# Attention stage: a reciprocal of 16 sums with a broadcast copy, and projections laid one to a slot

## The reference

```python
q = (x @ Wq + bq) ...; k = (x @ Wk + bk) ...; v = (x @ Wv + bv) ...
scores = einsum('bhqd,bhkd->bhqk', q / sqrt(32), k) + attention_bias
scores = where(src_mask, -inf, scores)
probs = softmax(scores, axis=-1)
ctx = einsum('bhqk,bhkd->bhqd', probs, v)
x = x + (ctx @ Wo + bo)
```

## Time and profile before

| | |
|---|---|
| time, median of 3 runs | 2644.94 us (2638.65 to 2649.93) |
| time of the profiled execution | 2651.21 us |
| span of the profiled execution | 2649.4 us |
| attention, first scores of the loop to the last transposes | 895.38 to about 1874.66 us |
| one middle batch (batch 1) | 1012.24 to 1135.09, 122.85 us |
| PE busy over the span | 92% |

### The profile page before, as it was taken

The page is one execution under the profiler, slowest core; times in us unless marked ns, Lnnn a source line. Parts: engine busy times, 40 slices in busy tenths (PEclk is TensorE's granted clock), DMA queues, the critical chain, the costliest instruction groups (busy, mean ns, idle before and its releaser), DMA issues. The chain is left out here.

```text
span 2649.4 us, 44273 instructions
## 1 busy us (share of the span) xinstructions
PE 2447.0 (92%) x16100; PEld 1920.0 (72%) x16100; DVE 1404.1 (53%) x2668; ACT 993.1 (37%) x1977; POOL 979.5 (37%) x806
## 2 busy tenths in 40 slices
PE   5999999999995789898989999998489999999999
PEld 4687787787783567676766667676378888888887
DVE  5354454454454677777677777777453333333322
ACT  4232231232230566666566656566231212111211
POOL 0031332332240565656565657666020122012200
PEclk9999999999997899999999999999789999999999
DMA  5201110110111555454555555545331001100100
GB/s 161 72 33 40 40 38 33 40 53 18 40 40 55 195 158 174 153 179 153 165 166 181 152 164 168 161 144 165 92 111 48 32 16 47 47 23 25 47 32 16
DMA packets 133361, 243.69 MB, mean 92 GB/s; under 512 B 13212, under 2 KB 17452, under 8 KB 133184
## 3 DMA queue, kind: packets, MB, share of 16 engines
q1 hardware_dynamic: 133184, 241.39, 28.4%
HBM read 216.17 MB, written 25.20 MB: 91 GB/s over the span
## 5 line engine op out<-in xcount | busy, mean ns | idle before, releaser
L951 POOL TENSOR_TENSOR at_bias<-at_bias,at_mask 128x512 f32<-128x512 f32 x512 | 587.3, 1173 | 381.0 <-DMA at_bias<-in_fside_Bx16xSxS 343.3
L648 DVE CAST L_hh<-L_hid 128x512 fp32r<-128x512 f32 x256 | 122.5, 478 | 797.9 <-PE L_acc L746 758.4
L487 ACT ACTIVATE L_hid<-L_turn,L_b1c 128x512 f32<-128x512 f32 x256 | 176.5, 690 | 983.9 <-PE L_turn L285 978.8
L283 PE MATMUL L_turn<-L_xth,L_w1h 128*128 128x512 f32 x1024 | 406.7, 397 | 7.7 <-ACT L_hid L487 5.4
L744 PE MATMUL L_acc<-L_w2h,L_hh 128*128 128x512 f32 x1024 | 403.1, 394 | 8.6 <-DVE L_hl L650 8.6
L284 PE MATMUL L_turn<-L_xth,L_w1l 128*128 128x512 f32 x1024 | 400.7, 391 | 0.0
L285 PE MATMUL L_turn<-L_xtl,L_w1h 128*128 128x512 f32 x1024 | 400.2, 391 | 0.0
L746 PE MATMUL L_acc<-L_w2l,L_hh 128*128 128x512 f32 x1024 | 400.1, 391 | 0.0
L745 PE MATMUL L_acc<-L_w2h,L_hl 128*128 128x512 f32 x1024 | 400.0, 391 | 0.0
L982 ACT ACTIVATE at_bias<-at_bias,at_neg_top 128x512 f32<-128x512 f32 x512 | 363.5, 714 | 44.3 <-DVE at_neg_top L1100 44.1
L1100 DVE CUSTOM_DVE_ANT_0 at_bias<-at_score,at_bias 128x512 f32<-128x512 f32 x512 | 333.0, 684 | 55.9 <-issue 29.8
(11 more groups left out here) (201 smaller groups left out, 3116.0 us busy)
## 6 DMA issues: line engine op xcount, KB each, us to landing
at_bias<-in_fside_Bx16xSxS SPq DMA_DIRECT2D x256, 512.0 KB, 3.7
L_xin<-in_x SPq DMA_DIRECT2D x8, 1024.0 KB, 5.4
L_xres<-in_x SPq DMA_DIRECT2D x8, 1024.0 KB, 5.4
at_xin<-x_scratch SPq DMA_DIRECT2D x8, 1024.0 KB, 6.5
at_xres<-x_scratch SPq DMA_DIRECT2D x8, 1024.0 KB, 6.9
L_xin<-x_scratch SPq DMA_DIRECT2D x8, 1024.0 KB, 5.5
L_xres<-x_scratch SPq DMA_DIRECT2D x8, 1024.0 KB, 5.5
x_scratch<-L_xres SPq DMA_DIRECT2D x7, 1024.0 KB, 4.3
```

The costliest lines, as they stand in the source:

```text
L283: nc_mm = pe.matmul(out, ah, bh, start=i == 0, stop=False)
L487: nc.scalar.activation(hid[m % 2][:, :], turn[m % 2][:, :], func, bias=b1c[:, m:m + 1]).then_inc(h_act, 1)
L951: nc.gpsimd.tensor_tensor(tile, tile, mask[:, m % TT, :], ALU.add).then_inc(masked, 1)
```

## The change

1. `inverse` becomes two instructions: a reciprocal of 128 x 16 sums into a new tile inv, and, after a wait of DVE on its own semaphore, a copy that repeats each of the 16 values 32 times into the 128 x 512 tile. PE's `over` waits on the copy (spread_set).
2. The tables: OUTS puts one output in slot 1, one in slot 2 and two in slot 3. The keys of head tile 1 move from slot 0 to slot 15 of the batch before (KEYS 15: (5, 0), for batch 0 ahead of the loop), its queries from slot 1 to slot 0. VALUES begin in slot 9, which had none, and leave slot 15.
3. TURNS goes. The four k slices of the next x are turned at the end of slot 7 (slice 0, turn[1]), behind unit 1 of slot 8 (slice 1, into gen) and at the end of slot 8 (slices 2 and 3, turn[0] and turn[1]); ACT's and DVE's `turn_hi` and `turn_lo` take their places in slots 8 and 9. Slot 9, which turned slices 2 and 3, now multiplies.

```diff
-    KEYS = {0: (1, 0), 1: (1, 1), 4: (2, 0), 5: (2, 1), 6: (3, 0), 7: (3, 1), 10: (4, 0), 11: (4, 1)}
-    OUTS = {2: (0, 1), 3: (2, 3)}
-    TURNS = {8: (0, 1), 9: (2, 3)}
-    VALUES = {12: 0, 13: 1, 14: 2, 15: 3}
+    KEYS = {0: (1, 1), 4: (2, 0), 5: (2, 1), 6: (3, 0), 7: (3, 1), 10: (4, 0), 11: (4, 1), 15: (5, 0)}
+    OUTS = {1: (0,), 2: (1,), 3: (2, 3)}
+    VALUES = {9: 0, 12: 1, 13: 2, 14: 3}
...
-                of = sums[:, phase * PHASE:(phase + 1) * PHASE].unsqueeze(2).to_broadcast([P, PHASE, HD])
-                nc.vector.reciprocal(spread, of).then_inc(inv_set, 1)
+                nc.vector.reciprocal(inv[:, :], sums[:, phase * PHASE:(phase + 1) * PHASE]).then_inc(inv_set, 1)
+                dve.wait_ge(inv_set, b * PHASES + phase + 1)
+                nc.vector.tensor_copy(spread, inv[:, :].unsqueeze(2).to_broadcast([P, PHASE, HD])).then_inc(spread_set, 1)
...
             def over(b, phase):
-                pe.wait_ge(inv_set, b * PHASES + phase + 1)
+                pe.wait_ge(spread_set, b * PHASES + phase + 1)
...
+                elif m == 8 and j == 1 and not last:
+                    pe.wait_ge(nat_lo, nat_count(b, 3, 1))
+                    turn_x(b + 1, 1, gen)
...
             scores(0, 0, True)
+            pe.wait_ge(v_out, TT - 1)
+            project(0, 1, 0, ALL, gen)
...
-                    if m in TURNS and not last:
-                        pe.wait_ge(pt_even, b * (UNITS // 2) + 2 * m + 2)
-                        pe.wait_ge(pt_odd, b * (UNITS // 2) + 2 * m + 2)
-                        for k in TURNS[m]:
-                            turn_x(b + 1, k)
                     if m % TT == TT - 1:
                         over(b, m // TT)
+                    if m == 7 and not last:
+                        pe.wait_ge(pt_odd, b * (UNITS // 2) + 2 * m + 2)
+                        turn_x(b + 1, 0, turn[1])
+                    if m == 8 and not last:
+                        pe.wait_ge(pt_even, b * (UNITS // 2) + 2 * m + 2)
+                        turn_x(b + 1, 2, turn[0])
+                        pe.wait_ge(pt_odd, b * (UNITS // 2) + 2 * m + 2)
+                        turn_x(b + 1, 3, turn[1])
```

More of the change, by code:

```diff
@@ L1005, in _ @@
             for k in range(KT):
-                turn_hi(0, k)
+                turn_hi(0, k, turn[k % 2])
             split_weights(1)
@@ L1025, in body @@
                     before = m - 1
+                    if m == 8 and not last:
+                        turn_hi(b + 1, 0, turn[1])
+                    if m == 9 and not last:
+                        turn_hi(b + 1, 2, turn[0])
+                        turn_hi(b + 1, 3, turn[1])
                     if before in KEYS:
@@ L1030, in body @@
                         elif not last:
[L1031 to L1034, removed]
+                            nat_hi_of(b + 1, tile - KT, query, gen)
+                    if m == 0:
+                        nat_hi_of(b, 1, 0, gen)
                     if before in VALUES and not last:
                         values(b + 1, 1 - odd, VALUES[before], gen)
-                    if m == 0 and not first:
-                        values(b, odd, TT - 1, gen)
                     after = following(b, m, last)
@@ L1042, in body @@
                         exp(*after, 0)
+                    if m == 8 and not last:
+                        turn_hi(b + 1, 1, gen)
+                    if after:
                         exp(*after, 1)
@@ L1144, in body @@
                     before = m - 1
+                    if m == 8 and not last:
+                        turn_lo(b + 1, 0, turn[1])
+                    if m == 9 and not last:
+                        turn_lo(b + 1, 2, turn[0])
                     if before in KEYS:
@@ L1149, in body @@
                         elif not last:
-                            nat_lo_of(b + 1, 0, query, gen)
+                            nat_lo_of(b + 1, tile - KT, query, gen)
+                    if m == 0:
+                        nat_lo_of(b, 1, 0, gen)
                     if before in OUTS and not first:
-                        output(b - 1, OUTS[before][1], gen)
-                    if before in TURNS and not last:
-                        turn_lo(b + 1, TURNS[before][0])
+                        output(b - 1, OUTS[before][-1], gen)
                     if after:
                         scores(*after, 0)
-                    if before in TURNS and not last:
-                        turn_lo(b + 1, TURNS[before][1])
+                    if m == 9 and not last:
+                        turn_lo(b + 1, 3, turn[1])
                     if after:
@@ L1169, in body @@
                         scores(*after, 2)
-                    if m in OUTS and not first:
+                    if m == 8 and not last:
+                        turn_lo(b + 1, 1, gen)
+                    if m in OUTS and len(OUTS[m]) == 2 and not first:
                         output(b - 1, OUTS[m][0], gen)
@@ L1314, in beside @@
                         gen_free(b, m, first)
-                    if j < 2:
+                    if len(OUTS[m]) == 1:
+                        output(b - 1, OUTS[m][0], some, gen)
+                    elif j < 2:
                         output(b - 1, OUTS[m][0], range(6 * j, 6 * j + 6), gen)
```

52 lines of the change are left out of this document (27 added, 25 removed).

## The result

| | |
|---|---|
| changed kernel, median of 5 | 2576.23 us (2573.42 to 2580.99) |
| kernel before, median of 5 in all | 2645.56 us (2638.65 to 2649.93) |
| ratio | 0.974, 95% interval 0.9721 to 0.9759 |
| profiled execution: time, span | 2573.42 us, 2571.6 us |
| attention, first scores of the loop to the last outputs' first matmul | 895.70 to 1796.51 us |

The change is 2.6% faster. The windows divide the gain: batch 0 takes 105.28 instead of 116.86 (11.6 less), batches 1 to 6 take 692.2 (1000.98 to 1693.20) instead of 744.3 (52.1 less), and batch 7 up to its outputs about 103.3 instead of 118.1 (14.8 less). They add up to 78.5; the other stages are as they were.

A forecast was written before the change was run, and what follows sets the result against it. PE was taken as the bound, with its idle and slow time to win. Gains of 59 + 12 + 10 = 81, less 12 for the clock, gave 69 us: 2582 profiled, 2576 on the median's scale, range 2555 to 2605.

The forecast's parts named there:

- the sum of 69: Whole run: 59 from six middle batches, 12 first batch, 10 last, less 12 for the clock, in us.
- Slots: Middle batch, added slot by slot: 113.0 us against 122.85, 9.9 less; slot 8's length follows DVE's work.
- The hand-over behind it: End of slot 8: PE starts the last slice 0.24 us after DVE's copy of unit 3.
- The reciprocal's stalls: Slots 3, 7, 11, 15: PE waits behind DVE's long reciprocal, 0.65, 1.31, 1.31 and 0.90, together 4.2 us a batch.
- only the reciprocal pays: Rival, chance 0.06: slots 8 and 9 come to the old 17.9 plus the projection; 36 us gained, 2609.
- No gain comes of the even laying itself: Slots 1 to 3: spreading outputs one, one and two only moves PE's work, since slot 2 had no idle time.
- The cover: Slots with a reciprocal: PE's queued matmuls hide up to 1.96 us of DVE work ahead of its unit 1 copy.
- The inverse itself: DVE's small reciprocal, wait and copy, four times a batch: 0.7 us, between 0.6 and 1.2, instead of 3.27.
- The clock: Slot 8: PE's thin work lets the granted clock fall in all seven batches, 1.7 us a time, 12 in all.
- The edges: First and last batch: 12 and 10 us gained, before the clock's price.
- Late bias tiles: Rival, chance 0.03: shorter slots leave too little time for bias loads, DVE's scores then PE's wait, and the run is slower.

The follow-up runs named there:

- the run with the low half moved: Changed kernel plus three unread matmuls in slot 8, with DVE's low half of slice 1 moved behind its copy of unit 3: 2560.98 us, ratio 0.9675.
- The filler run: Three matmuls whose result nobody reads added to the changed kernel in slot 8 behind unit 3: 2565.31 us, ratio 0.9693.

## Why the prediction was right, point by point

- **The total.** 2576 against 2576.23. That it fits to 0.3 us is luck. By the profiled executions the forecast was 2582 and the measurement 2573.4, so the sum of 69 was 9 short; with the second profiled execution of the changed kernel (span 2576.4) it is 4 short. With the clock's 1.7 taken off each batch that has a slot 8, the forecast was 10.3 for batch 0, 48.8 for batches 1 to 6 and 10 for batch 7, and the windows gave 11.6, 52.1 and 14.8: every part was low.
- **Slots.** Slots 3, 7, 8, 9, 11 and 15 were forecast at 10.1, 7.7, 8.3, 6.8, 7.19 and 7.19 and came at 9.98, 7.44, 8.28, 6.78, 7.01 and 7.01; a middle batch at full clock at 113.0 and came at 112.35. Following DVE through slot 8 from the earlier trace rows gave start and end within 0.05 us (0.79 and 7.63 against 0.75 and 7.6), and the run with the low half moved shows that this chain ends the slot. The hand-over behind it was forecast at 0.24 and took 0.06, the last slice at 0.52 and took 0.59.
- **The reciprocal's stalls** were mis-sized. "Length less busy gives the same stall" summed to 4.2 us a batch; the same four slots gave 5.0 with the reciprocal alone, and slots 8 and 9 another 0.7 in the mean, 5.8 in all (6.4 in batch 1). A stall costs 0.2 to 0.3 more than its idle time, since the profile's busy time of the matmul ahead of the wait reaches past the point where the next one could start, and the slow stretch of slots 8 and 9 shortens. The same 0.2 is why slots 7, 11 and 15 were each forecast 0.2 too long.
- **So the rival "only the reciprocal pays"** was priced at 2609 and would have been 2597. Two thirds of the gain, some 50 us, is the reciprocal, and one third, some 25, the layout.
- **"No gain comes of the even laying itself"** is wrong. With the outputs and keys as before, 12 us of the layout's 25 are gone. The step behind that sentence looked for idle time in slot 2 and found none, and did not ask what the empty slot costs: one without a projection goes down to 5.8, not to 4.0. The sum was not hurt, since it was made slot by slot with slot 15 full.
- **The cover** was there, but 1.75 us and not 1.96: it was worked out as 3.27 less the idle 1.31, and the stall really cost 1.50. The inverse itself was mis-sized. It was forecast at 0.7, between 0.6 and 1.2; to the end of its copy it took from 0.7 to 1.8 us, over 1.2 in 13 of 32, since the copy was taken to lie between 0.42 and 0.68 and took 0.86 in the median and up to 1.55. The longest, 1.75 from start to start (slot 11 of batch 2), just used up the cover: that slot took 7.05 instead of 7.01. So the miss cost nothing.
- **The clock.** Forecast to fall in all seven batches for 1.7 us each, 12; it fell fully in three and partly in two, for 2.35 and 1.3, 9.7. In the second profiled execution it fell in all seven, as forecast, for 13.6 (slots 8 and 9 took 119.0 us, against seven times 15.06). The filler run gives 11 for having it up throughout. The mechanism was right, and so was the size within what differs from one execution to the next; that a batch can keep the clock was not foreseen. The Trainium skill says in "TensorE: Matmul & The Clock Gate", "Part 4: PE-mode transpose", that a transpose does not count as PE activity the way a matmul does. By it the clock would have fallen every time. The trace agrees only in part: in slot 8 of batch 1 PE did nothing but transposes from 1059.79 to 1066.15 and the granted clock stayed at 1.00, so here the measurement decides against the rule's strong form, though three matmuls more did keep the clock up every time.
- **The edges.** Batch 0 won 11.6 for 12. Batch 7 won 14.8 for 10: beside what was counted, its slot 13 had 3.06 us of waiting for nothing that the profile shows before and 0.97 after. In the other runs this wait is 0.74 to 0.97 us with the short inverse, 1.48 with the longer one and 1.90 with the old reciprocal in the new layout, so it goes with the length of the inverse two slots earlier. By what way stays open.
- **Late bias tiles** did not appear: POOL's waits for DMA fell from 343.3 to 270.8 us, and DVE's scores waited for POOL once, 0.8 us (before: seven times, 3.3 us).

## What to carry to other kernels

When two engines hand work over through a few banks, a slot without heavy work does not shrink to its own work: it ends by the hand-overs, and on PE it can cost the clock for the slot behind it as well. So lay the heavy work one to a slot, and cut a projection so that part of it fills the thin slot; that was worth 21 us on top of this change. Read the inner chain of the second engine start to start to find a thin slot's length, and count a stall of PE by distances of starts, since its idle time leaves a little out. A broadcast belongs behind the expensive operation, not in front of it.

## What the runs showed that I had not expected

- A DVE copy from SBUF to SBUF takes 0.427 us alone and 0.86 in the median beside POOL's additions of 1.18 us, up to 1.55; with POOL's additions cut to 8 columns the median is 0.427. The longest one (1197.29 to 1198.84) ended 0.29 us after a POOL instruction had ended at 1198.55, and so did the others: 31 of the 32 began while POOL was busy, and each ended 0.2 to 0.3 us after the POOL instruction then under way. So the copy waits for that instruction. The Trainium skill has a rule on it, in "Perfetto Trace Analysis", "Optimizing Scalar/DVE Operations": GpSimd and VectorE share an SBUF read port, and a two-port VectorE operation locks it for itself. The trace agrees that the two do not run side by side, with 0.43 us added in the median; here it is the copy that waits. The row of the mask operation did not warn of it, since its 0.417 is the median of operations most of which ran while POOL was idle: of the 28 that are made inside the batches, the 21 beside an idle POOL took 0.41 to 0.42, and the seven beside a busy one 0.42 to 1.53.
- A reciprocal takes about 6.3 ns for each further element a partition here, also where its source repeats the same sums: 0.248 us for 16, 1.153 for 160, 3.348 for 512 elements.
- At the start of batches 3 and 5, where the loop's body begins again, PE stands still for 2.0 to 4.7 us in every kernel here, and the profile shows nothing that it waits for (2.60 and 2.29 before, 2.57 and 2.54 after). The slot ahead is longer by that, and the granted clock is then mostly 0.79 or 0.80 in the next one, which takes 8.1 us instead of 6.6. The change does not touch these 4 us a time.
